# The row-maximum term of the attention scores: 32 rows, four products side by side, once per two key tiles

## The reference

```python
h = _layernorm(x, axis=-1) * (1 + ca) + sa
q = (h @ Wq)  -> 16 heads of 64;  k, v = h @ Wk, h @ Wv -> 4 heads of 64, each used by 4 q heads
q, k = q*cos + rotate_half(q)*sin, k*cos + rotate_half(k)*sin
attn = q @ k.T / sqrt(64) + slopes[head] * (key - query)      # 1024 x 1024 per head, no mask
attn = softmax(attn, axis=-1)
x = x + ga * ((attn @ v) @ Wo)
```

## Time and profile before

| what | value |
|---|---|
| median of three runs | 1103.88 us |
| the profiled execution's own time | 1104.65 us |
| its span | 1102.8 us |
| busy: TensorE, VectorE, POOL, ScalarE | 95%, 75%, 72%, 65% |
| stretch with the 32 heads | about 103.5 to 690 us of the span |

### The profile page before, as it was taken

How to read it: one execution, slowest core, us unless ns; L and a number is a source line. 1 busy time by engine, 2 the same in 40 slices (tenths; PEclk the granted TensorE clock), 3 DMA queues, 4 the chain that set the end, 5 groups by cost and what they waited for, 6 DMA issues and landing times. The chain is left out here.

```text
span 1102.8 us, 23118 instructions
## 1 busy us (share of the span) xinstructions
PE 1050.2 (95%) x8304; PEld 652.5 (59%) x8304; DVE 825.1 (75%) x1490; ACT 712.9 (65%) x1285; POOL 791.3 (72%) x542
## 2 busy tenths in 40 slices
PE   7985999999999999999999999889999897999988
PEld 3662555555555555555555555766777694777778
DVE  7975676767666666666666664689999689999876
ACT  3663676767676767676767665048877656888754
POOL 3873678778777877787778778679996338666526
PEclk9995999999999999999999999999999999999999
DMA  8697123204132232141322100101111100111111
GB/s 267 212 285 235 37 50 78 58 30 107 30 79 58 59 78 59 31 106 34 83 57 51 39 13 21 39 11 33 34 44 35 25 2 17 36 35 34 36 29 34
DMA packets 71744, 71.70 MB, mean 65 GB/s; under 512 B 31396, under 2 KB 56528, under 8 KB 71632
## 3 DMA queue, kind: packets, MB, share of 16 engines
q1 hardware_dynamic: 71632, 70.23, 24.0%
HBM read 44.65 MB, written 15.85 MB: 55 GB/s over the span
## 5 line engine op out<-in xcount | busy, mean ns | idle before, releaser
L923 DVE CUSTOM_DVE_ANT_0 junk<-psum,alibi 128x1024 bf16<-128x1024 f32 x256 | 312.7, 1222 | 194.2 <-PE psum L995 186.5
L888 ACT ACTIVATE E<-psum,keybias_sb 128x1024 f32<-128x1024 f32 x256 | 277.8, 1112 | 189.6 <-PE psum L1019 175.2
L805 POOL TENSOR_TENSOR sum_p<-sum_p,E 128x1024 f32<-128x1024 f32 x96 | 232.8, 2425 | 84.4 <-ACT E L888 79.8
L1031 PE MATMUL psum<-E,V 128*64 128x512 f32 x1024 | 248.0, 605 | 0.0
L995 PE MATMUL psum<-KH,QH 64*128 64x512 f32 x512 | 118.6, 459 | 11.6 <-PEq L292 6.0
L1031 PEld LDWEIGHTS psum<-E,V 128*64 128x64 f32 x1024 | 62.1, 136 | 112.3 <-issue 106.4
L995 PEld LDWEIGHTS psum<-KH,QH 64*128 64x128 f32 x512 | 49.4, 189 | 120.5 <-DVE M L923 84.2
L1019 PE MATMUL psum<-QH,KH 64*128 64x512 f32 x512 | 102.2, 395 | 2.2 <-DMA QM<-mrow 2.2
L813 POOL TENSOR_TENSOR sum_p<-sum_p,xpos_sb 128x1024 f32<-128x1024 f32 x32 | 76.5, 2390 | 38.2 <-DVE xpos_sb L933 38.2
L1019 PE MATMUL psum<-QL,KH 64*128 64x512 f32 x512 | 101.5, 392 | 0.0
L1019 PE MATMUL psum<-QH,KL 64*128 64x512 f32 x512 | 101.4, 392 | 0.0
(11 more groups left out here) (155 smaller groups left out, 2087.2 us busy)
## 6 DMA issues: line engine op xcount, KB each, us to landing
qa_scratch<-tQ SPq DMA_DIRECT2D x8, 1024.0 KB, 5.3
QH<-qa_scratch SPq DMA_DIRECT2D x32, 256.0 KB, 3.6
QH<-qa_scratch SPq DMA_DIRECT2D x64, 128.0 KB, 3.5
vp_att<-v_att SPq DMA_DIRECT2D x64, 128.0 KB, 2.3
XF<-inverse_scratch SPq DMA_DIRECT2D x30, 256.0 KB, 3.4
KH<-k_scratch SPq DMA_DIRECT2D x16, 256.0 KB, 4.2
KL<-k_scratch SPq DMA_DIRECT2D x16, 256.0 KB, 5.2
v_scratch<-v_sb SPq DMA_DIRECT2D x16, 128.0 KB, 4.5
```

The source lines that it names most:

```text
L805: pool.tensor_tensor(sum_p[:, s, :], first, E[:, k % 4, :], ALU.add)\
L888: act.activation(E[:, k % 4, :], scores(k % 2), ACT.Exp, bias=kb).then_inc(exp_done, 1)
L923: dve.tensor_tensor_reduce(junk[:, :], banks(max_bank(i, k), 2), alibi[:, s, :], -1.0, BIG, ALU.add, ALU.min, M[:, s, k:k + 1]).then_inc(m ...
L1031: last = pe.matmul(banks(6 + i % 2)[HD * ch:HD * ch + HD, :], V[:, g, k, :], E[:, k % 4, ch * 512:(ch + 1) * 512], start=(k == 0), stop=(k ...
```

## The change

The maximum term leaves `qk_step` and becomes a step of its own for two key tiles, ahead of their scores. It contracts over 32 rows instead of 64. Its four matmuls (first and second 512 queries, for tile k and for tile k+1) use the four groups of 32 rows of the array and write four different banks. QM therefore carries its rows four times, at partitions 0, 32, 64 and 96, brought by four DMAs instead of two. Because the step writes the banks of both tiles, it waits for the exponentials of both tiles before. On ScalarE the bias row moves from behind tile 5 to behind tile 6.

```diff
-                        for ch in range(2):
-                            sp.dma_start(QM[HD * ch:HD * ch + 1, s, :]...
+                        for n in range(4):
+                            ch = n % 2
+                            sp.dma_start(QM[32 * n:32 * n + 1, s, :]...
...
-                    need(act, ld_m[s], 32 * (i // 2))
+                    need(act, ld_m[s], 64 * (i // 2))
...
-                            if k == 5 and i + 3 < HEADS:
+                            if k == 6 and i + 3 < HEADS:
                                 alibi_row(i + 3, (i + 3) % 2)
...
+                    def m_step(i, k):
+                        if k == 0:
+                            need(pe, ld_m[i % 2], 64 * (i // 2 + 1))
+                        need(pe, exp_done, TB * i + k)
+                        if i == 0 and k == 0:
+                            pe.wait_ge(qm_filled, 3)
+                            pe.wait_ge(max_done, LEAD)
+                        for n in range(4):
+                            rows = slice(32 * n, 32 * n + 32)
+                            pe.matmul(scores(n // 2)[:, n % 2 * 512:(n % 2 + 1) * 512], one_rows[rows, :], QM[rows, i % 2, :],
+                                      start=True, stop=False)
...
                     def qk_step(i, k):
                         if k == 0:
-                            need(pe, ld_m[i % 2], 32 * (i // 2 + 1))
                             need(pe, ql_done, i + 1)
-                        need(pe, exp_done, TB * i + k - 1)
-                        if i == 0 and k < 2:
-                            pe.wait_ge(qm_filled, 3)
-                            pe.wait_ge(max_done, LEAD - 1 + k)
-                        terms = (..., (KL[:, g, keys], QH[:, s]), (one_rows[:, :], QM[:, i % 2]))
+                        terms = (..., (KL[:, g, keys], QH[:, s]))
-                                                 start=(n == 0), stop=(n == len(terms) - 1))
+                                                 start=False, stop=(n == len(terms) - 1))
...
                     def head(i):
                         for k in range(0, TB, 2):
+                            m_step(i, k)
                             qk_step(i, k)
                             qk_step(i, k + 1)
```

More of the change, by code:

```diff
@@ L723, in load_m @@
                         need(sp, mrow_done, i + 1)
-                        for ch in range(2):
-                            sp.dma_start(QM[HD * ch:HD * ch + 1, s, :].bitcast(F32).rearrange("p (t c) -> p t c", c=P),
+                        for n in range(4):
+                            ch = n % 2
+                            sp.dma_start(QM[32 * n:32 * n + 1, s, :].bitcast(F32).rearrange("p (t c) -> p t c", c=P),
                                          mrow[TB // 2 * ch:TB // 2 * (ch + 1), s, :].bitcast(F32)).then_inc(ld_m[s], 16)
@@ L1006, in qk_step @@
                         if k == 0:
-                            need(pe, ld_m[i % 2], 32 * (i // 2 + 1))
                             need(pe, ql_done, i + 1)
-                        need(pe, exp_done, TB * i + k - 1)
-                        if i == 0 and k < 2:
-                            pe.wait_ge(qm_filled, 3)
-                            pe.wait_ge(max_done, LEAD - 1 + k)
                         keys = slice(k * P, (k + 1) * P)
-                        terms = ((KH[:, g, keys], QH[:, s]), (KH[:, g, keys], QL[:, s]), (KL[:, g, keys], QH[:, s]),
-                                 (one_rows[:, :], QM[:, i % 2]))
+                        terms = ((KH[:, g, keys], QH[:, s]), (KH[:, g, keys], QL[:, s]), (KL[:, g, keys], QH[:, s]))
                         for n, (key, query) in enumerate(terms):
```

## The result

The changed kernel takes 1134.82 us (median of four, 1133.22 to 1136.17) against 1104.46 us for the kernel before; the recorded ratio is 1.0261, 95% interval 1.0241 to 1.0281. One of the four runs before took 4587.57 us; the other three lie at 1103.51 to 1105.04, and the ratio leaves it out. The two medians as they stand give 1.0275, inside the interval. It is slower by 29 to 30 us. The forecast was 1129 us, with a range of 1098 to 1146.

A forecast was written before the change was run, and what follows sets the result against it. TensorE's own steps were taken as the bound: per pair of tiles -0.46 + 0.23 + 2 x 0.20 = +0.17 us, +21.8 over 128; with +2 wait and +1.4 start, +25 us, 1129 us forecast, range 1098 to 1146.

The forecast's parts named there:

- The bound and the removed work: TensorE's own steps set the time; two pairs of maximum-term matmuls go per pair of tiles, 0.46 us.
- The group at one step: On TensorE, four 32-row matmuls run side by side as one added step, 0.23 us per pair of tiles.
- Rival 3: The group's four products run in twos, another 0.23 us per pair of tiles: 1158 us, chance 0.04.
- The changes of shape: On TensorE, two added changes between 64 and 32 rows per pair of tiles, 0.20 us each (gap 0.09, load 0.11).
- rivals 1 and 2: 1: 32 and 64 rows are no change of shape, 1085 us, chance 0.15; 2: only one part paid, 0.12.
- rival 2: Per change of shape only the gap or only the unhidden load is paid: 1099 to 1108 us, chance 0.12.
- The earlier wait: Next head's first group waits for tile 7's exponential, delayed by the bias row: 0.06 us in 29 heads, +2 us.
- The start: In the first head nothing hides the four DMAs of QM's rows: +1.4 us, once.
- The DMAs later on: In later heads QM's four DMAs and the loads queued behind them on SyncE stay hidden: no cost.

The follow-up runs named there:

- e6: e1 with VectorE's maximum taken over the second half of the keys only, as control of e5: 1127.59 us, ratio 1.0202 to the kernel before.
- e1: The changed kernel with the bias row back behind tile 5: 1131.16 us, ratio 1.0216 to the kernel before.
- e10: The kernel before with only the bias row moved behind tile 6: 1106.15 us, ratio 1.0003.
- e4: e1 with the group of four 32-row products computed twice, the second over the first: 1157.93 us, ratio 1.0470 to the kernel before.
- e8: e1 with the group split, two 32-row products ahead of each key tile's scores: 1209.77 us, ratio 1.0940 to the kernel before.
- e2: e1 with the group's four products over 64 rows in two pairs, and two DMAs into QM: 1107.12 us, ratio 1.001 to the kernel before.
- e3: e1 with the 32-row group one place earlier, between V and the maximum product: 1137.48 us, ratio 1.0278 to the kernel before.
- e9: e3 with the bias row behind tile 7 instead of tile 5: 1136.49 us, ratio 1.0279 to the kernel before.
- e5: e3 with VectorE's maximum taken over the second half of the keys only: 1105.99 us, ratio 1.0008 to the kernel before.

## Why the prediction was right

**The bound and the removed work.** Right. The loss is the length of TensorE's steps, and the engines with room enter little: VectorE only at the start (below) and not later (e6), ScalarE only by the wait below (e1, e10). No run changes POOL's work.

**The group at one step.** Right: 0.23 us by e4. Rival 3 (in twos) is out.

**The changes of shape, the step that decided.** Right. I had taken the price from changes of row count between 128 and 64, and 64 to 32 costs the same: 0.20 us by e8, gap 0.09 and unhidden load 0.11. With no such change left, in e2, the loss is gone, and rivals 1 and 2 are out. That the sum is met so well is in part luck: the heads of e1, which has the changes without the wait, take 22.0 us more than before (602.3 less 580.3), where I had 21.8. In the middle heads a pair of tiles costs +0.19 us and not +0.17 (a head of e1 is 19.03 us long, one before 18.29), which would be 24 us over 128 pairs. Two things that I had not seen make up most of the difference. The first pair takes 0.3 us less than before (5.78 against 6.11); why, no run shows. And the last five groups have no maximum product ahead of them, since that pass is through: there the V block is followed by the group at once, with one added change instead of two. One pair there, from start to start of its scores, in the kernel before and in the changed one:

```profile
674.41 0.51 PE L1019 MATMUL psum<-QH,KH 64*128 64x512 f32 x2
...
678.35 0.50 PE L1019 MATMUL psum<-QH,KH 64*128 64x512 f32 x2
```

```profile
704.13 0.51 PE L1027 MATMUL psum<-QH,KH 64*128 64x512 f32 x2
...
708.04 0.50 PE L1027 MATMUL psum<-QH,KH 64*128 64x512 f32 x2
```

The three such pairs of the two traces that lie side by side take 3.92, 3.90 and 3.94 us before and 3.90, 3.89 and 3.91 in the changed kernel: with one change for the saved step a pair is 0.02 us shorter, and the prices say 0.03 (-0.46 + 0.23 + 0.20). That is the price of a change read once more, in the changed kernel itself.

**The earlier wait.** Its place and cause were right (tile 0 of the next head, the exponential of tile 7, delayed by the bias row), its size was low: 0.18 us a head instead of 0.06. The group was due at 508.74 + 0.43 = 509.17; its weight load started at 509.32 and its matmuls at 509.35. In 29 heads that is 5.2 us instead of 2, and the stretch of the heads says the same (607.5 less 602.3). Two terms did it. The exponential ended 5.04 us after the first maximum product instead of 5.00, and from its end to the waiting matmul it took 0.14 us, 0.11 of it to the weight load (509.21 to 509.32), where I had taken 0.04.

**The start.** The size was about right, 1.24 us by the distance from the last maximum product of the lead to the first product into the scores' banks, the group in the changed kernel (100.55 to 103.53 before, 100.86 to 105.08 after) against 1.4, and the cause was wrong. I had put it on the four DMAs. The first group waits for the 12th maximum:

```profile
103.70 1.22 DVE L924 CUSTOM_DVE_ANT_0 junk<-psum,alibi 128x1024 bf16<-128x1024 f32 x1
104.86 0.08 DVE L924 DVE_READ_ACCUMULATOR2_ANT M<- 128x1 f32 x1
...
105.05 0.32 PEld L1015 LDWEIGHTS psum<-QM,one_rows 32*128 32x128 f32 x4 [3.90 <-DMA QM<-mrow]
105.08 0.80 PE L1015 MATMUL psum<-QM,one_rows 32*128 32x512 f32 x4 [3.43 <-DVE M L924]
```

The maximum ends at 104.94 and the group starts at 105.08. The view names the DMA for the weight load and the maximum for the matmul; e2 decides, since with two DMAs it starts 4.22 us after its last maximum product as well (100.75 to 104.97). It is the waiting for both tiles' banks that costs it, not the DMAs. The group's own step ahead of the first scores is 0.73 us there (105.08 to 105.81) instead of 0.44, at the lower level of the clock (granted 0.50 from 100 to 107 us).

**The DMAs later on** were hidden, as forecast. Whether they reached e3's earlier group isn't shown: the view says so, and e9, where they are issued 1.06 us earlier against it (3.17 instead of 2.11 us ahead of the second maximum product: 505.10 to 508.27, in e3 504.34 to 506.45), is no faster.

Together 22.0 + 5.2 + 1.2 + 0.7 = 29 us, where I had 25. The difference of the two spans is 31.6: another 0.3 lies before the first maximum products, and 2.2 behind the last scores, where the two kernels are the same. From the last high-by-high score product to the end it is 418.9 us before and 421.1 in the changed kernel, and 417.1 to 421.1 over all twelve traces, so that these 2.2 us are no effect of the change.

One slip in the working: the lower end of rival 2 is 1101 us by its own terms (-6 + 2 + 1.4), not 1099. No chance rests on it.

## What to carry to other kernels

Count how often the array's shape changes in the order, not only the steps: here two changes cost 0.40 us and the packing of four small products saved 0.23, so small-row packing pays only where more than 0.40/0.23, say two, steps are saved for each pair of changes (an estimate from these two prices), or where the neighbours have the same shape, as in e4. Moving a step to save a change also moves its neighbours closer to one another; check what each waits for from another engine (e3: 1.77 us of VectorE's round trip against 1.74 us for six steps). A wait on TensorE costs its own length and also the weight load that would have been hidden (in e3 0.09 and 0.11 us).

## What the runs showed of the hardware

The price of a change didn't depend on which dimension changed. From 64 to 32 rows and back (e8) the gap is 0.09 us and the unhidden load 0.11. From 128*64 to 64*128 in the changed kernel, and from 128*64 to 32*128, rows and columns at once, in e5, the V block takes 1.87 us to the next start, and that start is followed 0.43 and 0.44 us later by another change. Four products in four row groups, into four PSUM banks, ran at the pace of one 64-row pair (0.23 us, e4). And a busy total can mislead: the row of the changed term fell by 36 us while the kernel lost 30.
